# Emptying query stacks first in steps 7 and 11 of a two-attention decoder layer, and moving key maxima and query rows on the SyncE queue

## Reference

```python
x = x + self_attention(layernorm(x))      # 16 heads of 8
x = x + cross_attention(layernorm(x), ctx, mask)
x = x + moe(layernorm(x))                 # 64 experts, 8 per token, and a shared one

# self_attention: q_in = x Wq + bq; Q = [q_in, conv3(q_in)] qproj; K likewise; V = x Wv + bv
scores = einsum('bhqd,bhkd->bhqk', Q, K) / sqrt(8)
scores = scores * tau[..., None] + delta[:, :, None, :]
out = softmax(scores) @ V @ Wo
# cross_attention: the same without convolutions, tau and delta; masked scores become -1e15
```

## Time and profile before

| | |
|---|---|
| median of 3 runs | 304.18 us (302.94, 304.18, 401.68) |
| the profiled execution | 303.79 us |
| its span, first to last instruction | 302.0 us |
| TensorE busy | 288.7 us, 96% of the span |
| VectorE, ScalarE, GpSimd busy | 76%, 63%, 61% |
| mean granted TensorE clock | 0.989 |

### The profile page before, as it was taken

How to read it: one execution, slowest core, us unless ns; L and a number is a source line. 1 busy time by engine, 2 the same in 40 slices (tenths; PEclk the granted TensorE clock), 3 DMA queues, 4 the chain that set the end, 5 groups by cost and what they waited for, 6 DMA issues and landing times.

```text
span 302.0 us, 5440 instructions
## 1 busy us (share of the span) xinstructions
PE 288.7 (96%) x1721; PEld 206.3 (68%) x1721; DVE 228.2 (76%) x513; ACT 191.3 (63%) x352; POOL 185.3 (61%) x259
## 2 busy tenths in 40 slices
PE   8999979999999999899889999999999999999995
PEld 3654756666655565456665788888888888888883
DVE  3698877799859886987896559789956676676664
ACT  2698827796884666466752797766655555555553
POOL 8430061098708870985177799999975666666661
PEclk9999968999999999999999999999999999999999
DMA  7702764457576243350000637766434353444311
GB/s 260 242 2 31 194 161 101 101 112 258 111 201 124 63 105 95 89 140 2 2 1 25 199 113 205 214 198 188 131 99 137 109 171 126 127 134 131 123 61 35
DMA packets 30636, 37.18 MB, mean 123 GB/s; under 512 B 5136, under 2 KB 19856, under 8 KB 30608
## 3 DMA queue, kind: packets, MB, share of 16 engines
q1 hardware_dynamic: 30608, 36.84, 43.0%
HBM read 28.43 MB, written 3.93 MB: 107 GB/s over the span
## 4 chain that ended last, share of the span: by engine, by line
PE 80%; DVE 10%; SPq 5%; ACT 2%; issue 2%; DMA 1%; ACTq 0%; DVEq 0%
PE bank L486 54%; PE bank L866 5%; PE bank L868 5%; PE bank L867 5%; PE bank L672 2%; SPq L391 2%; PE bank L647 2%; PE bank L690 2%; SPq L379 1%; PE bank L659 1%; DVE conv L1232 1%; DVE conv L1230 1%; PE bank L695 1%; PE bank L492 1%; PE bank L656 1%
## 5 line engine op out<-in xcount | busy, mean ns | idle before, releaser
L1864 POOL TENSOR_TENSOR qbd<-vs,qbd 128x512 fp32r<-128x512 f32 x65 | 83.8, 1291 | 33.3 <-ACT qbd L1175 33.2
L486 PE MATMUL bank<-khl,stacks 128*128 128x512 f32 x396 | 101.5, 392 | 1.9 <-DVE vs L1659 1.9
L486 PEld LDWEIGHTS bank<-khl,stacks 128*128 128x128 f32 x396 | 73.5, 188 | 18.7 <-issue 3.7
L1690 DVE TENSOR_TENSOR conv<-bank,conv 128x512 f32<-128x512 f32 x60 | 41.5, 692 | 31.4 <-ACT bank L1139 28.2
L1139 ACT ACTIVATE bank<-bank 128x512 f32<-128x512 f32 x61 | 35.5, 582 | 43.9 <-PE bank L486 43.9
L1298 DVE TENSOR_REDUCE rawmax<-bank 128x4 f32<-128x512 f32 x64 | 43.3, 684 | 10.9 <-PE bank L486 10.0
L1175 ACT ACTIVATE qbd<-vs 128x512 fp32r<-128x512 f32 x65 | 40.6, 624 | 7.1 <-DVE vs L1667 4.6
L486 PE MATMUL bank<-stacks 128*128 128x512 f32 x96 | 42.2, 488 | 2.8 <-DMA stacks<-stacks 2.0
L1698 DVE TENSOR_TENSOR vs<-conv,bank 128x512 f32<-128x512 f32 x61 | 41.9, 687 | 2.1
L1063 ACT ACTIVATE conv<-bank 128x512 f32<-128x512 f32 x64 | 35.1, 596 | 7.0 <-PE bank L486 6.3
L1828 POOL TENSOR_TENSOR stacks<-ring,stacks 128x384 fp32r<-128x384 f32 x33 | 33.6, 1020 | 1.4
(11 more groups left out here) (239 smaller groups left out, 440.9 us busy)
## 6 DMA issues: line engine op xcount, KB each, us to landing
conv<-coefficient_rows SPq DMA_DIRECT2D x122, 128.0 KB, 2.9
ring<-w SPq DMA_DIRECT2D x33, 192.0 KB, 3.6
stacks<-stacks SPq DMA_DIRECT2D x68, 64.0 KB, 2.1
split_rows<-stacks SPq DMA_DIRECT2D x6, 256.0 KB, 3.4
stacks<-split_rows SPq DMA_DIRECT2D x16, 96.0 KB
split_rows<-khl SPq DMA_DIRECT2D x3, 512.0 KB, 4.3
stacks<-split_rows SPq DMA_DIRECT2D x8, 192.0 KB
pa<-pack_a SPq DMA_DIRECT2D x1, 706.0 KB, 5.4
```

The costliest lines, as they stand in the source:

```text
L486: return pe.matmul(out, lhsT, rhs, start=start, stop=stop)
L1690: dve.tensor_tensor(out, gate, spread[:, n % ROWS, :, :], ALU.mult).then_inc(gate_scaled, 1)
L1864: pool.tensor_tensor(hlo[:, n % 4, :].rearrange("p (b t) -> p b t", b=4), hx[n % 4], hhi[:, n % 4, :].bitcast(F32).rearrange("p (b t) -> p ...
```

## The change

Four things move; nothing is added or left out.
1. On SyncE the eight copies of maxima leave the head of the program and go behind the key rows that step 7 loads; the three stores of query rows (`put_rows(1)`) go behind the key loads of step 1.
2. On TensorE `sum_bias(0)` goes from ahead of the second `compose` to behind the first convolution.
3. On TensorE in steps 7 and 11, `second_stack(2)` stands ahead of the first scores of the next step, and the last transposed scores of the step stand behind all scores of the next.
4. In the same steps ScalarE copies the first stack ahead of `copy_o` and the third ahead of the third exponential; VectorE takes the third maximum ahead of `norm`.

```diff
@@ sync
                 if s == 7:
                     sp.wait_ge(rows_put[2], 48)
                     get_rows(2, kst[1], 0, 4, range(J))
+                    sp.wait_ge(kst_filled, G)
+                    get_maxima(0)
+                    get_maxima(4)
...
-            sp.wait_ge(kst_filled, G)
-            get_maxima(0)
-            get_maxima(4)
             sp.wait_ge(khi_ready, 2)
             sp.wait_ge(klo_ready, 2)
             put_rows(0, khl[0], 4, K_PARTS)
-            sp.wait_ge(qhi_ready, 2)
-            sp.wait_ge(qlo_ready, 2)
-            put_rows(1, qhl, 4, Q_PARTS)
...
+                if s == 1:
+                    sp.wait_ge(qhi_ready, 2)
+                    sp.wait_ge(qlo_ready, 2)
+                    put_rows(1, qhl, 4, Q_PARTS)
                 move_rows(s)
@@ tensor
             turn_inputs(0, 0, bank[0])
-            sum_bias(0, "qp2T", "cqb", "bq")
             compose(1)
...
                 if c == 0:
+                    sum_bias(0, "qp2T", "cqb", "bq")
                     sum_bias(1, "kp2T", "ckb", "bk")
...
                 if making is not None:
+                    second_stack(making, 2)
                     scores(s + 1, 0)
-                    second_stack(making, 2)
                 if now:
                     scoresT(s, 2)
                 if making is not None:
                     scores(s + 1, 1)
                     second_stack(making, 3)
+                    turn_out(s - 1)
+                    scores(s + 1, 2)
+                    scores(s + 1, 3)
                 if now:
                     scoresT(s, 3)
-                if making is not None:
-                    turn_out(s - 1)
-                if making is not None:
-                    scores(s + 1, 2)
-                    scores(s + 1, 3)
@@ scalar
+                if making is not None:
+                    second_stacked(making, 0)
                 if s >= 1:
                     copy_o(s - 1)
                 if s in (0, 2):
                     delta_weights(s // 2)
-                if making is not None:
-                    second_stacked(making, 0)
                 if s < STEPS:
                     exponential(s, 0)
                     exponential(s, 1)
+                if making is not None:
+                    second_stacked(making, 2)
                 if inputs is not None:
                     copy_inputs(1, inputs, 7)
                 if s < STEPS:
                     exponential(s, 2)
-                if making is not None:
-                    second_stacked(making, 2)
@@ vector
                     second_stacked(c, 3)
+                    maximum(s + 1, 2)
...
                 if ahead and not early:
-                    maximum(s + 1, 2)
                     maximum(s + 1, 3)
```

## The result

| | changed kernel, first set | changed kernel, second set | kernel before, beside them |
|---|---|---|---|
| median, us | 309.43 (307.71 to 311.94, 4 executions) | 310.79 (309.86 to 311.63, 4) | 303.91; 303.81 |
| ratio to before | 1.0199 [1.0106, 1.0292] | 1.0229 [1.0209, 1.0249] | |
| profiled execution, span | 307.71, 305.9 | 311.63, 309.8 | 303.79, 302.0 |

The change makes the kernel 5.5 us slower in the first set and 7.0 in the second; 307.5 had been forecast, with a range of 304.4 to 309.6; the median of the second set lies above the range. Both are needed.

What follows compares the result with a forecast made beforehand. The prediction took the kernel as TensorE-bound, losing time where TensorE waits for SyncE's key loads. Its terms, -1.8 + 4.0 + 1.2 + 0.2 = +3.6 on the profiled 303.79 us, gave 307.4, stated as 307.5, range 304.4 to 309.6.

Steps and rivals of the forecast that it cites:

- What bounds the kernel, and the sign: TensorE is 80% of the chain; its waits for SyncE's key loads in steps 1 and 8 decide; the kernel gets slower.
- Head, -1.8: Step 1: key loads start at 35.05, not 36.87, so TensorE's wait of 1.98 goes: -1.8 us (between 1.5 and 2.0).
- Bias sums, 0: At the head, eight small products only move inside a stretch where TensorE is fully busy: 0.
- Copies behind the key rows, landed at 87.7: Step 7: the copies run after the key rows in the queue, not beside them, and land at 87.7.
- The rival, ports side by side: Step 7: copies run beside the key rows, landing by 82.5 to 84.8; total 302.3 to 304.3 us, chance 0.17.
- Loads of step 8, a wait of 3.2: Key loads land at 91.7, TensorE waits 3.2 us ahead of step 8's scores; L659 there +3.1.
- Loads of step 9, landed at 96.9: Key loads follow step 8's by 5.2 us, land at 96.9 and put L659 of step 8 at 97.6: +4.0.
- The clock, +1.2: Between the scores of steps 8 and 9, half clock after TensorE's stand makes 96.9 into 98.1: +1.2 us.
- the later of two waits decides: The waits for the loads of steps 8 and 9 do not add; the later one sets the cost, +4.0.
- New order, 0: Steps 7 and 11: L659 does not move, as VectorE's work is the same: 0, at most 0.3 gained.
- GpSimd +0.2: Fourth exponential of step 7 ends 1.3 to 1.7 us later against GpSimd's slack of 1.0: 0 to +0.7, taken as +0.2.
- the prediction's "worse" case: Both loads late, half clock into step 9, GpSimd's inputs late too: +6 to +8, 309.5 to 312 us, chance 0.07.

Runs made afterwards that it cites:

- copies_at_head: The changed kernel with the eight copies of maxima back at the head of SyncE's queue, all else as changed: 303.86 us, ratio 0.9988.
- bias_split: copies_at_head with the key bias sum moved behind the second convolution, the query bias sum staying behind the first: 302.22 us, ratio 0.9949.
- bias_alone: The kernel before with only the query bias sum moved behind the first convolution: 303.35 us, ratio 0.9984.
- rows_at_ten: The changed kernel with the key rows of step 9 moved behind the loads of step 10: 307.88 us, ratio 1.0141.
- weights_after: The changed kernel with the five weight loads of step 8 moved to step 9: 312.14 us, ratio 1.0275.
- changed_again: The changed kernel itself, unedited, run for a second set of executions and a second profile: 310.79 us, ratio 1.0229.
- copies_only: The kernel before with only the eight copies of maxima moved to step 7; query rows, bias sums and order untouched: 308.89 us, ratio 1.0158.
- half_bias_back: The changed kernel with four of the eight copies back at the head and the query bias sum at its old place: 306.54 us, ratio 1.0081.
- bias_back_again: The changed kernel with the query bias sum back at its old place, repeated beside the changed kernel: 308.43 us, ratio 1.0149.

## Why the forecast went wrong, and where it held

- **What bounds the kernel, and the sign: right.** Time is lost where TensorE waits for SyncE's queue, at the two places named, and in some executions at a third.
- **Head, -1.8: right in size, wrong in its cause.** L659 of step 0 moves by 1.94 and that of step 1 by 2.24. But the eight copies need not leave: moving the three stores gives -1.7 by itself, with the copies where they were. The text had both numbers for it (the stacked keys are complete at 35.01; three stores take half of the issues from 32.04 to 36.87) and did not ask which edit was needed.
- **Bias sums, 0: the first of two steps that failed.** "Only moved inside a full stretch" counts TensorE's time and not what the instructions are. Sixteen 128x1 products in a row brought half clock for 3.41 us near 17.5 in five of the eight profiles of kernels that have them, and in none of the nine of kernels that do not. It put step 0 later by 1.8 between copies_at_head and bias_split (1.6 in the medians). In the changed kernel it was worth 0.9 and 2.4 in the two pairs, and nothing with four copies (305.98 against 306.54) or where a load had set the end (bias_alone). Not each execution shows it: the first profile of the changed kernel, rows_at_ten and weights_after do not.
- **Copies behind the key rows, landed at 87.7: right.** They landed at 85.95 (the chain has 6.64 us of transfer from 79.31) on a timeline that is 2.2 earlier, so at 88.1 on that of before; 0.42 of the engines and 55 GB/s. (The prediction's 0.51 and 76 GB/s for the copies at the head include the first stores behind them: from 26.0 to 32.0 alone it is 0.44 and 62.) The rule of the Trainium skill ("DMA: Bandwidth & Descriptors", section "Queues, rings and completion order") that a ring is served in order agrees with this trace: 7.04, 11.68 and 15.07 us with no, four and eight copies. The rival, ports side by side, is out: 160 GB/s with the rows, then 55 with the copies alone.
- **Loads of step 8, a wait of 3.2:** 3.85 and, in changed_again, 3.17.
- **Loads of step 9, landed at 96.9: too early by 1.6.** They landed at 96.33, which is 98.5 on the clock of before. They need 5.1 us from first issue and not 4.0, behind five weight loads.
- **The clock, +1.2: mechanism seen, size by luck.** The half clock came (3.41 us from 89.94), and the chain to L660 of step 8 goes through it. But the loads of step 9, late by 1.6, would have set L660 at 97.18, only 0.19 earlier, so the clock added 0.2 there. In copies_only, with the old order and no stand for the loads of step 9, it lasted 6.83 us and the step took 17.07, 1.60 more. Two errors cancelled in the first profile: +5.2 forecast for this step, +5.9 measured; by the estimate of 97.18, 5.7 of it are the loads' (4.0 forecast) and 0.2 the clock's (1.2).
- **Loads of step 10: the second step that failed, a term the sum did not have.** The text held that the later of two waits decides, and stopped there. But each late load makes SyncE issue the next later, and the key rows of step 9 stand ahead of the third. It cost 1.75 and 1.5 of half clock in changed_again, as much in half_bias_back, and nothing in the first profile. Why it comes in one execution and not in another is open.
- **New order, 0, and GpSimd +0.2: right.** 1.001 [0.9999, 1.0021]; GpSimd starts 1.34 later where 1.3 to 1.7 was forecast, and 0.5 from step 10 to 11 is set against 0.3 gained in step 8. In the changed kernel, whose steps before are longer, GpSimd costs nothing: step 10 to 11 takes 7.03, before 7.04.

The sum was +3.6 and the profiled execution of the first set showed +3.9, partly by luck: it is the fastest, has neither the half clock near 17.5 nor the third stand, and hides the two errors of step 8. The medians showed +5.5 and +7.0. What the forecast lacked can be read from the two profiles of before and changed_again (times 7.84 apart):

| stretch, by L659 or L660 | forecast | changed_again |
|---|---|---|
| up to step 7 | -1.8 | -0.33 |
| step 7 to 8 | +5.2 | +4.71 |
| step 8 to 9 | 0 | +1.83 |
| step 9 to 10 | 0 | +1.51 |
| step 10 to 11 | +0.2 | -0.01 |

Its time lies where the prediction's "worse" case had 309.5 to 312 with a chance of 0.07, but by another way: that case had GpSimd's inputs late, and they were not. The medians of the experiments make a chain from before to the changed kernel: query rows alone -1.7; from there to bias_back_again, that is copies to step 7 and the new order, +6.4 (308.43 - 302.03); bias sum +2.4. That these give +7.1, the whole, follows from how they are taken and confirms nothing.

Open: why the loads of step 10 needed at most 7.4 us from first issue in one execution (95.75 to 103.13) and 8.7 in another (96.90 to 105.58) with the same transfers ahead of them. Whether the half clock at 40 after the head, there in some profiles without any wait, has one cause was not tried.

## What to carry to other kernels

When an in-order queue is full, a transfer moved into it costs every load behind it: follow the delay through all loads until one has slack, not through the first two. Ask of each edit in a bundle whether the gain needs it; here three stores gave it all, and the eight copies were free where they stood. Putting tiny matmuls in one row is no free move: here full products between them kept the clock.

## What the hardware showed

- Sixteen 128x1 products in a row (14.97 to 16.76 in copies_at_head) on a TensorE that never stood, with full products ahead and behind, were followed by 3.41 us at 1.2 GHz, from 17.61. So it was in five of eight profiles. With eight, a convolution and eight the mean clock was 1.0 in four executions of five.
- After a stand the clock is not certain to fall: 3.79 us brought no half clock in weights_after, 3.85 brought 3.41 us in the first profile, and 4.34 brought 6.83 in copies_only.
- A copy of 8 partitions and 64 KB takes 1.0 us of the queue behind other transfers as one of eight, and 1.2 as one of four.
